# Four graph layers over one 2048-node adjacency: diagonal products of the first and fourth chunk one place later, the mask counts and row checks set apart, and S2 before S3 in the second column block

## The chip, the cores and the metric

The kernel runs on one core of a Trainium2 chip (trn2). The time is the device time of one execution in microseconds (us). Three runs of the kernel before gave 1041.26, 1042.79 and 1042.98 us, median 1042.79 us. TensorE is called PE, VectorE DVE, ScalarE ACT, GpSimd POOL and SyncE SP.

## The reference, cut to what matters

Activations `x` are 8 batches x 2048 nodes x 64 channels; `adj` is a 2048 x 2048 row-normalised 0/1 matrix. Four layers follow each other, each with a residual and a layer norm:

```python
x = ln(x + L0(x))     # Chebyshev: x, A x, 2 A (A x) - x, times per-node weights
x = ln(x + L1(x))     # attention masked by adj > 0.5
x = ln(x + L2(x))     # ((A + I) (x W^T + b)) / rowsum
v = x with node 0 replaced
for _ in range(3):    # L3
    v = relu([v, A v] W1^T + b1) W2^T + b2
x = ln(x + v)
```

No entry of this `adj` is above 0.5, so every attention row is a uniform mean over the nodes. The kernel uses that and proves it while it runs: it counts the mask entries per row, compares them with the count of entries in the rows of `adj` as read from memory, looks for entries above the diagonal's value, and branches to a general program when anything differs. A count, a check and a branch are therefore part of the computation.

## The kernel before, in words

**Data.** The 512 columns (batch x channel) are four chunks `c` of 128; the 2048 nodes are four blocks `j` of 512. `Bm` holds the mask as fp8, `S` the stationary operand as a high and a low fp16 half, `T` the results as high and low halves, `X` the running activations in fp32. Every fp32 tensor that PE reads is split in two steps: ACT copies it to fp16 (high half), then POOL or DVE writes the rest (low half).

**Order.** Nothing is scheduled at run time. Two Python functions, `middle_order` and `last_order`, make one list of steps, and each engine walks through it and does its own part of each step, waiting on semaphores. So a step early in the list stands in front of everything after it on *each* of its engines. In `last_order`, `at(y, ...)` puts steps at half product number y: products `P` 1 to 15 have two halves each, and the steps of y = 2k stand before the first half of product k, those of 2k + 1 before its second. From y = 32 on the places are the half slots h = y - 32 of the last layer (`on(h, ...)`).

**The steps that the change and the prediction touch.**
- `P k` (L788): a 512-column product of layer 2, 32 matmuls of 512 columns, k = 4c + j, and 8 small ones (L938). Product k uses PSUM bank k mod 3.
- `E k`: ACT copies the bank to T (high half), DVE makes the low half. `W c j` (L773 to L775, 12 matmuls) is the weight product; it waits for the low half of E k with k = 4c + j, and stands at y = 2k + 4 (2k + 6 for c = 0), so between two products: `W 1 0` (needs E4) before product 6, `W 1 1` (E5) before 7, `W 1 2` (E6) before 8, `W 1 3` (E7) before 9, `W 2 0` (E8) before 10.
- `split c j`: after DVE has scaled a block (`apply`, L1531), ACT copies it to fp16 and POOL makes the low half.
- `rows`: eight small DVE operations on per-row constants.
- `v0 c j`: the same split for the third pass of the last layer's input; `D c j` (L763, L764, 8 matmuls) multiplies that input by the diagonal matrix `dg` and waits for POOL's low half.
- `G`, `M`, `t22`, `V`: the last layer as one level of a seven-product block scheme with slots `X11, X12, S2, S1, S3, S4, X22`. `G` is a weight product, `M` the product with the mask (L955), `mix` makes the sums S1 to S4 on DVE (L1598), `cut` splits each into halves on ACT and POOL.
- `chk it` (16 of them): ACT copies row tile `it` of the mask, 128 x 2048 fp8, with an accumulated sum into `cnt`. `sgn it` (16): ACT makes two passes over a row tile of `adj` in fp32: Relu (over the diagonal) with its sum into `over`, then Sign with its sum into `sg1`. There is one landing buffer `rowt` for those rows, which SP refills (1 MB) after each Sign, and one scratch output `junk`, which `chk` and the Relu share.
- `flags`, `total`, `verdict`: DVE, PE and DVE again turn the sums into the branch flag. The branch stands before h = 56.

Before, one list entry `chk` and one `sgn` alternate: `chk` at y = 12, 16, 20, 24, 28, 32, then every 4 less a little; `sgn` two places after each. The last `sgn` is at h = 40, `flags` at 44, `total` at 46 and `verdict` at 47.

Of the kernel before, what the change touches and what calls it, by code (L numbers as in the profile page):

```python
# [177 lines left out]
def last_order(after):  # L178


    order = []
    late, half, between = {}, {}, {}

    def at(y, *steps):

        (late if y < 32 else half).setdefault(y if y < 32 else y - 32, []).extend(steps)

    def on(h, *steps):
        half.setdefault(h, []).extend(steps)

    for k in sorted(after):
        at(int(2 * k), *after[k])
    for c in range(NC):
        for j in range(4):
            y = 2 * (4 * c + j)
            at(y + (6 if c == 0 else 4), ("W", c, j))
            at(y + (8, 6, 6, 5)[c], ("sq", 2, c, j), ("red", 2, c, j))
        y = (15, 21, 31, 36)[c]
        at(y, ("var", 2, c))
        at(y + 1, ("root", 2, c), ("rs", 2, c), ("apply", 2, c, 0), ("apply", 2, c, 1), ("v0t", c))  # L200
        at(y + 2, ("apply", 2, c, 2), ("apply", 2, c, 3), ("v0", c, 0))
        at(y + 3, ("v0", c, 1), ("v0", c, 2))
        at(y + 4, ("v0", c, 3))
        y += c > 0
        at(y + 5, ("D", c, 0), ("D", c, 1))
        at(y + 6, ("D", c, 2), ("D", c, 3))
    at(8, ("rows",))
    for i in range(48, 64):
        at(i - 46, ("bt", i))

    for n, y in ((2, 26), (3, 40)):
        at(y, *take(n, 0, "X11", "X12"))
        at(y + 1, cut(n, 0, "X11"), *take(n, 1, "X11", "X12"), cut(n, 0, "X12"))
        at(y + 2, cut(n, 1, "X11"), cut(n, 1, "X12"))
    for n, y in ((2, 29), (3, 45)):
        at(y, *take(n, 0, "X21", "X22"))
        at(y + 1, *mixes(n, 0, 1, 3, 2), cut(n, 0, "X22"), cut(n, 0, "S2"))
        at(y + 2, cut(n, 0, "S3"), *mixes(n, 0, 4), *take(n, 1, "X22"), cut(n, 0, "S1"))
        at(y + 3, cut(n, 0, "S4"), *take(n, 1, "X21"))
        at(y + 4, *mixes(n, 1, 1, 3, 2), cut(n, 1, "X22"), cut(n, 1, "S2"))  # L220
        at(y + 5, *mixes(n, 1, 4), cut(n, 1, "S1"))
        at(y + 6, cut(n, 1, "S3"), cut(n, 1, "S4"))
    for it in range(NT):
        at(12 + 4 * it if it < 5 else 32 + 4 * (it - 5) - (it - 5) // 4, ("chk", it))
        at(14 + 4 * it if it < 5 else 34 + 4 * (it - 5) - (it - 5) // 4, ("sgn", it))
    for k in range(16):
        p = pieces("P", k)
        order += late.pop(2 * k, []) + (p[0:2] if k else []) + late.pop(2 * k + 1, []) + (p[2:4] + [("E", k)] if k else [])
    for n in (4, 5, 6, 7):
        h = 14 * (n - 3)  # L230
        on(h + 2, *take(n, 0, "X11"))
        on(h + 3, *take(n, 0, "X12"), cut(n, 0, "X11"))
        on(h + 4, *take(n, 0, "X21"), cut(n, 0, "X12"))
        on(h + 5, *take(n, 0, "X22"))
        on(h + 6, *mixes(n, 0, 1, 3, 2), cut(n, 0, "X22"))
        on(h + 7, cut(n, 0, "S2"), *mixes(n, 0, 4), *take(n, 1, "X11"))
        on(h + 8, cut(n, 0, "S4"), cut(n, 0, "S1"), *take(n, 1, "X22"))
        on(h + 9, cut(n, 1, "X11"))
        on(h + 10, cut(n, 0, "S3"), *take(n, 1, "X12"))
        on(h + 11, cut(n, 1, "X12"), *take(n, 1, "X21"))  # L240
        on(h + 12, *mixes(n, 1, 1, 3, 2), cut(n, 1, "X22"))
        on(h + 13, cut(n, 1, "S2"), *mixes(n, 1, 4))
        on(h + 14, cut(n, 1, "S1"))
        on(h + 15, cut(n, 1, "S3"))
        on(h + 16, cut(n, 1, "S4"))
    on(44, ("flags",))
    on(46, ("total",))
    on(47, ("verdict",))

    for n, s, jj, h in ((6, 1, 0, 61), (6, 1, 1, 62), (6, 4, 0, 69), (6, 4, 1, 70), (6, 5, 0, 71), (6, 5, 1, 72), (6, 6, 0, 72),  # L250
                        (6, 6, 1, 73), (7, 1, 0, 75), (7, 1, 1, 76), (7, 4, 0, 80), (7, 4, 1, 81)):
        on(h, ("F", *ending(n, s, jj)), ("sq", 3, *ending(n, s, jj)))
    def outs(n, s):
        return [("out", *ending(n, s, jj)) for jj in range(2)]

    for n, s, h in ((6, 1, 64), (6, 4, 71), (6, 5, 74), (6, 6, 75), (7, 1, 77)):
        u = ending(n, s, 0)
        on(h, ("var3", *u), ("root3", *u), ("rs3", *u), *outs(n, s))

    r, (u, v), (x, y) = ending(7, 4, 0), [ending(7, 5, jj) for jj in range(2)], [ending(7, 6, jj) for jj in range(2)]  # L260
    on(82, ("var3", *r), ("root3", *r), ("F", *u), ("sq", 3, *u), ("rs3", *r), *outs(7, 4))
    on(83, ("F", *v))
    between[83] = [("F", *x), ("sq", 3, *v), ("red", 3, *v), ("var3", *u)]
    on(84, ("root3", *u), ("rs3", *u), *outs(7, 5), ("F", *y), ("sq", 3, *x), ("red", 3, *x), ("sq", 3, *y), ("red", 3, *y), ("var3", *x), ("root3", *x),
       ("rs3", *x), *outs(7, 6))
    on(57, ("fin",))
    for h in range(85):
        if h == 56:
            order.append(("branch",))
        order += half.get(h, [])  # L270
        if h < 84:
            n, s, jj = 2 + h // 14, h % 14 // 2, h % 2
            if s == 3:
                order.append(("t22", n, jj))
            order += [("M", n, s, 2 * jj)] + between.get(h, []) + [("M", n, s, 2 * jj + 1), ("V", n, s, jj)]
    return order
# [16 lines left out]
def cut(n, jj, what):  # L293
    return "cut", n, jj, what
# [7 lines left out]
def gnn_kernel(nc, x_in, at_in, a_in, embt_in, sm_in, bx_in, w0_in, a12_in, w0bb_in, out):  # L302
    ctx = ExitStack()
    with ctx:
# [376 lines left out]
                    RSN[norm_key(x)] = len(RSN)  # L681

        number_norms()

        ORDER3 = [ending(n, s, jj) for n in (6, 7) for s in ENDS for jj in range(2)]

# [379 lines left out]
        def scalar_steps(e, steps):  # L1066
# [3 lines left out]
            for step in steps:  # L1070
# [91 lines left out]
                elif kind == "cut":  # L1162
                    n, jj, what = step[1:]
                    if what[0] == "X":
                        e.wait_ge(s_ut, GN[(n // 2, *block_of(n, jj, what))] + 1)
                    else:
                        e.wait_ge(s_mx, MN["mix", n, jj, what] + 1)

                    if what in ("S1", "S2", "S3"):
                        if n > 2:  # L1170
                            e.wait_ge(s_p, slot_done(n - 1, {"S2": 2, "S1": 3, "S3": 4}[what], 1))
                    elif n >= 4:
                        e.wait_ge(s_p, slot_done(n - 2, [x[0] for x in SLOTS].index(what), 1))
                    else:
                        c, j = block_of(n, jj, "X21" if what == "S4" else what)
                        e.wait_ge(s_d, 4 * c + j + 1)
                    fn(half_of(n, what, 0, jj), four(made(n, jj, what)), ACT.Copy).then_inc(s_uh, 1)
                elif kind == "v0":
                    c, j = step[1:]
                    e.wait_ge(s_p, 4 * c + 4)  # L1180
                    e.wait_ge(s_n[2], 4 * c + j + 1)
                    if j == 0:
                        e.wait_ge(s_vt, c + 1)
                        fn(stile(0, 0, c), V0T, ACT.Copy)
                        fn(S[:, 0, 1:4, chunk(c)], X[:, 1:4, chunk(c)], ACT.Copy).then_inc(s_vh, 1)
                    else:
                        fn(spart(0, c, j), xpart(c, j), ACT.Copy).then_inc(s_vh, 1)
                elif kind == "D":
                    c, j = step[1:]
                    e.wait_ge(s_d, 4 * c + j + 1)  # L1190
                    fn(T[:, c, 0, block(j)], bank(aux_bank[step]), ACT.Copy, scale=1.0 / EDGE).then_inc(s_dh, 1)
                elif kind == "chk":
                    it = step[1]
                    e.wait_ge(s_zp, 8 * NT)
                    if it:
                        e.wait_ge(s_over, it)
                    fn(junk, Bm[:, it, :], ACT.Copy, accum_out=cnt[:, it:it + 1]).then_inc(s_cnt, 1)
                elif kind == "sgn":

                    it = step[1]  # L1200
                    e.wait_ge(s_land, 16 * (it + 1))
                    e.wait_ge(s_nr, 1)
                    e.wait_ge(s_cnt, it + 1)
                    fn(junk, rowt, ACT.Relu, bias=nr[:, it:it + 1], accum_out=over[:, it:it + 1]).then_inc(s_over, 1)
                    e.wait_ge(s_over, it + 1)
                    fn(rowt, rowt, ACT.Sign, bias=nr[:, it:it + 1], accum_out=sg1[:, it:it + 1]).then_inc(s_sign, 1)

# [1054 lines left out]
```

## Time and profile before

| | before |
|---|---|
| device time, median of 3 (us) | 1042.79 |
| profiled execution: time (us) | 1043.06 |
| profiled execution: span of the profile (us) | 1041.3 |
| mean granted PE clock, share of full | 0.994 |
| PE busy / DVE / ACT / POOL (us) | 1012.3 / 678.1 / 456.8 / 552.9 |
| share of the span | 97% / 65% / 44% / 53% |

The span runs from the first to the last instruction; 1.8 us lie around it. Busy shares are averages over stages with different limits. PE is busy nearly always, so what can move the time is a stretch in which PE stands still, or in which its clock is lower. ACT is busy for 44% of the whole, and that share differs much from stage to stage.

### The profile page before, as it was taken

How to read it: one execution, taken by the hardware profiler on the slowest of the kernel's cores; microseconds unless marked ns; L12 is line 12 of the kernel's file. 1: busy time of each engine (PE TensorE's matmuls, PEld its weight loads, DVE VectorE, ACT ScalarE, POOL GpSimd, SP SyncE). 2: the span in 40 equal slices, each digit the busy share in tenths (PEclk: the TensorE clock that was granted, in tenths of full speed). 3: DMA queues.
4: the chain of work that ended last, by engine and by line, in shares of the span. 5: the costliest groups of instructions: out<-in, count | busy, mean ns of one | idle time of the engine just before them, and what ended most of it. 6: DMA issues, size and time to landing. Idle time of an engine off the chain costs nothing. (4 is left out here: it accounts for less than half of the span.)

```text
span 1041.3 us, 18648 instructions
## 1 busy us (share of the span) xinstructions
PE 1012.3 (97%) x6854; PEld 486.3 (47%) x6854; DVE 678.1 (65%) x1683; ACT 456.8 (44%) x1109; POOL 552.9 (53%) x645
## 2 busy tenths in 40 slices
PE   7999999999999999999999999999999999999995
PEld 3445444444444444434445556454554545455553
DVE  4877565657566786687667775776584545547556
ACT  4632323333334543444333575584766532232632
POOL 0005497766658798879878374464443242323311
PEclk9999999999999999999999999999999999999998
DMA  9930000000000000000010121121221100000022
GB/s 371 404 127 1 2 1 2 1 2 1 1 1 2 2 1 2 1 2 1 1 42 1 41 82 42 41 82 41 82 82 50 72 1 2 3 2 21 21 62 61
DMA packets 14658, 45.65 MB, mean 44 GB/s; under 512 B 960, under 2 KB 9280, under 8 KB 10080
## 3 DMA queue, kind: packets, MB, share of 16 engines
q1 hardware_dynamic: 14560, 44.39, 11.5%
q8 instruction: 56, 0.92, 0.4%
q14 instruction: 42, 0.34, 0.1%
HBM read 40.19 MB, written 4.19 MB: 43 GB/s over the span
## 5 line engine op out<-in xcount | busy, mean ns | idle before, releaser
L788 PE MATMUL PS<-BW,S 128*128 128x512 fp8e4 x1280 | 291.9, 380 | 0.7 <-DVE R L1219 0.7
L1068 ACT ACTIVATE T<-PS,SM 128x128 f32<-128x128 f32 x384 | 112.8, 365 | 234.3 <-DVE X L1219 155.9
L918 PE MATMUL PS<-WZ,R 64*128 64x512 f16 x1536 | 198.0, 377 | 1.2 <-ACT T L1068 1.2
L788 PEld LDWEIGHTS PS<-BW,S 128*128 128x128 f16 x1280 | 120.6, 98 | 150.3 <-issue 18.2
L955 PE MATMUL PS<-BW,S 128*128 128x512 fp8e4 x768 | 173.1, 379 | 0.6 <-POOL T L1737 0.6
L1737 POOL TENSOR_TENSOR T<-T 128x128 f32<-128x128 f32 (+1 forms) x192 | 124.3, 647 | 74.4 <-ACT T L1068 64.3
L1219 DVE SCALAR_TENSOR_TENSOR X<-PS,SM,X 128x128 f32<-128x128 f32 x320 | 109.5, 342 | 76.4 <-PE PS L918 76.4
L918 PEld LDWEIGHTS PS<-WZ,R 64*128 64x128 f16 x1536 | 69.5, 94 | 104.1 <-issue 26.3
L955 PEld LDWEIGHTS PS<-BW,S 128*128 128x128 f16 x768 | 73.7, 98 | 83.9 <-issue 1.1
L955 PE MATMUL PS<-BW,T 128*128 128x512 fp8e4 x480 | 109.5, 379 | 1.3 <-POOL T L1737 1.3
L1737 POOL TENSOR_TENSOR S<-R,S 128x512 f16<-128x512 f32 (+1 forms) x46 | 52.3, 1144 | 105.6 <-ACT S L1068 105.5
L1219 DVE SCALAR_TENSOR_TENSOR T<-PS,SM,T 128x128 f32<-128x128 f32 x256 | 87.7, 343 | 27.1 <-PE PS L918 27.1
L918 PE MATMUL PS<-WZ,T 64*128 64x512 f16 x768 | 103.8, 376 | 0.0
L1737 POOL TENSOR_TENSOR T<-R,T 128x512 f16<-128x512 f32 x40 | 49.3, 1240 | 87.6 <-DVE T L1211 44.8
L1219 DVE SCALAR_TENSOR_TENSOR R<-PS,cs,R 128x512 f32<-128x512 f32 x48 | 36.0, 749 | 64.1 <-PE PS L955 32.7
L1761 POOL TENSOR_TENSOR BW<-BW 128x512 fp8e4<-128x512 fp8e4 x64 | 70.9, 1113 | 2.7
L955 PEld LDWEIGHTS PS<-BW,T 128*128 128x128 f16 x480 | 46.2, 98 | 54.4 <-POOL T L1737 1.8
L1219 DVE SCALAR_TENSOR_TENSOR R<-PS,ra,R 128x128 f32<-128x128 f32 x176 | 48.8, 342 | 33.6 <-PE PS L775 21.8
L1068 ACT ACTIVATE R<-PS,cs 128x512 f32<-128x512 f32 x48 | 32.6, 679 | 83.7 <-PE PS L782 52.5
L1068 ACT ACTIVATE WZ<-WZ,ra 128x2048 f16<-128x2048 f32 (+1 forms) x32 | 63.9, 1996 | 1.3 <-DMA WZ<-a_in 0.8
L1737 POOL TENSOR_TENSOR X<-X,T 128x128 f32<-128x128 f32 x128 | 58.4, 457 | 10.0
L773 PE MATMUL PS<-hat,T 128*128 128x128 f16 x320 | 57.8, 221 | 4.2 <-DVE T L1219 2.5
(210 smaller groups left out, 1518.9 us busy)
## 6 DMA issues: line engine op xcount, KB each, us to landing
WZ<-a_in SPq DMA_DIRECT2D x16, 1024.0 KB, 4.8
BW<-at_in SPq DMA_DIRECT2D x8, 1024.0 KB, 18.4
R<-at_in SPq DMA_DIRECT2D x7, 1024.0 KB, 12.7
out<-X SPq DMA_DIRECT2D x16, 256.0 KB, 2.3
X<-x_in SPq DMA_DIRECT2D x3, 1024.0 KB, 19.6
T<-w_in SPq DMA_DIRECT2D x1, 1536.0 KB, 15.4
R<-at_in SPq DMA_DIRECT2D x2, 512.0 KB, 4.7
SM<-sm_in SPq DMA_DIRECT2D x1, 520.5 KB, 17.9
```

The costliest lines, as they stand in the source:

```text
L773: e.matmul(ok, th, hat[:, 0, kind, :], start=True, stop=False)
L788: m = e.matmul(o, stile(h, t, c), Bm[:, t, block(j)], start=(t == 0 and h == 0), stop=(last and t == NT - 1 and h == 1))
L918: m = e.matmul(bank(b0 + q), halves[kd][zh][r, :], WZ[r, wh, kd, block(g)], start=(i == 0), stop=(i == 8))
L955: m = e.matmul(o, half_of(n, what, h, q % 2)[:, t, :], b[:, 4 * (q % 2) + t, :], start=(s in (0, 1, 3) and q % 2 == 0 and t == 0 and h == ...
L1068: return e.activation(o, i, f, **kw)
L1219: return e.scalar_tensor_tensor(out=o, in0=a, scalar=s, in1=b, op0=f, op1=g)
L1737: return e.tensor_tensor(o, a, b, f)
L1761: e.tensor_tensor(o, a, b, f, saturate=False).then_inc(s_bt, 1)
```

## The change

Four edits, and no instruction is added or taken away:

1. `D` of chunk 0 moves from y = 20, 21 to 21, 22, and `D` of chunk 3 from y = 42, 43 to 43, 44.
2. The list entry `sgn` is cut into `ovr` (the Relu pass) and `sgn` (the Sign pass). All 16 `chk` go to y = 2 to 17, one at each half product. `ovr` 0 to 3 go to y = 10, 13, 16, 19, `ovr` 4 to 15 to y = 51 to 79 (every 2 or 3 places), and each `sgn` one place after its `ovr`. `number_junk` lets each pass that writes `junk` wait for the one before it in the list.
3. In the second column block (jj = 1) of pairs n = 2 and 3, DVE makes S2 before S3, and S2 is cut before X22.
4. `flags`, `total` and `verdict` move from h = 44, 46, 47 to 49, 51, 52.

```diff
-        y += c > 0
+        y += (1, 1, 1, 2)[c]
         at(y + 5, ("D", c, 0), ("D", c, 1))
         at(y + 6, ("D", c, 2), ("D", c, 3))
...
-        at(y + 4, *mixes(n, 1, 1, 3, 2), cut(n, 1, "X22"), cut(n, 1, "S2"))
+        at(y + 4, *mixes(n, 1, 1, 2), cut(n, 1, "S2"), *mixes(n, 1, 3), cut(n, 1, "X22"))
...
-        at(12 + 4 * it if it < 5 else 32 + 4 * (it - 5) - (it - 5) // 4, ("chk", it))
-        at(14 + 4 * it if it < 5 else 34 + 4 * (it - 5) - (it - 5) // 4, ("sgn", it))
+        at(2 + it, ("chk", it))
+        y = 10 + 3 * it if it < 4 else 51 + (13 * (it - 4)) // 5
+        at(y, ("ovr", it))
+        at(y + 1, ("sgn", it))
...
-    on(44, ("flags",))
-    on(46, ("total",))
-    on(47, ("verdict",))
+    on(49, ("flags",))
+    on(51, ("total",))
+    on(52, ("verdict",))
...
+        def number_junk():
+            held = None
+            for x in TAIL:
+                if x[0] in ("chk", "ovr"):
+                    JUNK[x] = held
+                    held = (s_cnt if x[0] == "chk" else s_over, x[1] + 1)
```

What this does to the instruction rows is shown at three places. All line numbers of the changed kernel are 16 higher there.

ACT from the end of the second layer's variances (128x32) on, before. `T<-PS` is an `E`, `S<-X` a `split`, `R<-X` the squares of a norm.

```order
L1068 ACTIVATE T<-T 128x32 [waits s_var] x2
L1068 ACTIVATE T<-PS 128x512 [waits s_p]
L1068 ACTIVATE S<-X 128x4x128 [waits s_n1,s_p2]
L1068 ACTIVATE T<-PS 128x512 [waits s_p]
L1068 ACTIVATE S<-X 128x4x128 [waits s_n1,s_p2]
L1068 ACTIVATE T<-PS 128x512 [waits s_p]
L1068 ACTIVATE S<-X 128x4x128 [waits s_n1,s_p2]
L1068 ACTIVATE R<-X 128x512 [waits s_y2]
L1068 ACTIVATE T<-PS 128x512 [waits s_p]
```

The same place of ACT in the change; `WZ,ra<-BW` is a `chk`.

```order
L1084 ACTIVATE T<-T 128x32 [waits s_var] x2
L1084 ACTIVATE WZ,ra<-BW 128x2048 [waits s_zp]
L1084 ACTIVATE WZ,ra<-BW 128x2048 [waits s_cnt,s_zp]
L1084 ACTIVATE T<-PS 128x512 [waits s_p]
L1084 ACTIVATE S<-X 128x4x128 [waits s_n1,s_p2]
L1084 ACTIVATE WZ,ra<-BW 128x2048 [waits s_cnt,s_zp] x2
L1084 ACTIVATE T<-PS 128x512 [waits s_p]
L1084 ACTIVATE S<-X 128x4x128 [waits s_n1,s_p2]
L1084 ACTIVATE WZ,ra<-BW 128x2048 [waits s_cnt,s_zp] x2
L1084 ACTIVATE T<-PS 128x512 [waits s_p]
```

Two counts stand now in front of each of E1, E2, E3 and E4, where there was none.

ACT from the exponential of the attention row (chunk 3) to E6, before.

```order
L1068 ACTIVATE ROW<-ROW 128x128 [waits s_neg]
L1068 ACTIVATE R<-X 128x512 [waits s_y2]
L1068 ACTIVATE T<-PS 128x512 [waits s_p]
L1068 ACTIVATE R<-X 128x512 [waits s_red,s_y1] x2
L1068 ACTIVATE R<-X 128x512 [waits s_red,s_y2]
L1068 ACTIVATE WZ,ra<-BW 128x2048 [waits s_zp]
L1068 ACTIVATE R<-X 128x512 [waits s_red,s_y1] x2
L1068 ACTIVATE T<-PS 128x512 [waits s_p]
```

The same place in the change; `WZ,ra<-WZ,ra` is an `ovr` or, with only s_over, a `sgn`.

```order
L1084 ACTIVATE ROW<-ROW 128x128 [waits s_neg]
L1084 ACTIVATE R<-X 128x512 [waits s_y2]
L1084 ACTIVATE WZ,ra<-WZ,ra 128x2048 [waits s_cnt,s_nr,s_land]
L1084 ACTIVATE WZ,ra<-BW 128x2048 [waits s_over,s_zp]
L1084 ACTIVATE WZ,ra<-WZ,ra 128x2048 [waits s_over]
L1084 ACTIVATE WZ,ra<-BW 128x2048 [waits s_cnt,s_zp]
L1084 ACTIVATE T<-PS 128x512 [waits s_p]
L1084 ACTIVATE R<-X 128x512 [waits s_red,s_y1] x2
L1084 ACTIVATE R<-X 128x512 [waits s_red,s_y2]
L1084 ACTIVATE WZ,ra<-BW 128x2048 [waits s_cnt,s_zp]
```

Four wide passes stand now between the exponential and E5, where there was none.

PE from the end of product 9 on, before: `dg` rows with s_vl are `D 0 0` and `D 0 1`, the `hat` row is `W 2 0`, and product 10 follows.

```order
L938 MATMUL PS<-dg,S 128x128 x8
L763 MATMUL PS<-dg,S 128x128 [waits s_vl,s_y2]
...
L763 MATMUL PS<-dg,S 128x128 [waits s_vl,s_y2]
...
L773 MATMUL PS<-hat,T 128x128 [waits s_hl,s_zl,s_y2]
...
L788 MATMUL PS<-BW,S 128x512 [waits s_sl,s_zl]
```

The same place in the change.

```order
L954 MATMUL PS<-dg,S 128x128 x8
L789 MATMUL PS<-hat,T 128x128 [waits s_hl,s_zl,s_y2]
...
L804 MATMUL PS<-BW,S 128x512 [waits s_sl,s_zl]
L804 MATMUL PS<-BW,S 128x512 x7
...
L779 MATMUL PS<-dg,S 128x128 [waits s_vl,s_y2]
```

`W 2 0` comes straight after product 9, and `D 0 0` only after the first half of product 10.

## Rows read from the trace of the kernel before

**Rows 1.** The page: busy us, share of the span and instructions of each engine.

```profile
PE 1012.3 (97%) x6854; PEld 486.3 (47%) x6854; DVE 678.1 (65%) x1683; ACT 456.8 (44%) x1109; POOL 552.9 (53%) x645
```

**Rows 2.** Timeline of PE: start us, us, engine line, [idle before <-releaser].

```profile
565.59 7.07 PE L788 MATMUL PS<-BW,S 128*128 128x512 fp8e4 x32
...
572.95 0.22 PE L773 MATMUL PS<-hat,T 128*128 128x128 f16 x1
...
573.62 7.07 PE L788 MATMUL PS<-BW,S 128*128 128x512 fp8e4 x32
...
596.57 0.61 PE L938 MATMUL PS<-dg,S 128*128 128x128 f16 x8
...
600.76 0.22 PE L763 MATMUL PS<-dg,S 128*128 128x128 f16 x1 [3.14 <-POOL S L1737]
...
602.29 4.87 PE L788 MATMUL PS<-BW,S 128*128 128x512 fp8e4 x16
...
607.89 3.62 PE L788 MATMUL PS<-BW,S 128*128 128x512 fp8e4 x16
```

**Rows 3.** Timeline of PE, 668 to 748 us: its four later stops.

```profile
668.49 0.23 PE L773 MATMUL PS<-hat,T 128*128 128x128 f16 x1 [1.69 <-DVE R L1219]
...
686.74 0.39 PE L780 MATMUL PS<-T,hat 128*128 128x512 f16 x1 [0.52 <-DVE T L1219]
...
706.09 0.23 PE L763 MATMUL PS<-dg,S 128*128 128x128 f16 x1 [1.39 <-DVE SM L1219]
...
747.26 1.90 PE L955 MATMUL PS<-BW,T 128*128 128x512 fp8e4 x8 [1.27 <-POOL T L1737]
```

**Rows 4.** Timeline of ACT: one count, and one Relu with its Sign.

```profile
569.39 1.90 ACT L1068 ACTIVATE WZ<-BW 128x2048 f16<-128x2048 fp8e4 x1
...
571.28 0.61 ACT L1068 ACTIVATE R<-X 128x512 f32<-128x512 f32 x1
...
577.40 1.99 ACT L1068 ACTIVATE WZ<-WZ,ra 128x2048 f16<-128x2048 f32 x1
...
579.51 2.00 ACT L1068 ACTIVATE WZ<-WZ,ra 128x2048 f32<-128x2048 f32 x1
```

**Rows 5.** Busy us of each engine in two stretches, with granted clock, DMA share, GB/s.

```profile
538.64:591.49 52.85, 52.85 (x357) 28.56 (x356) 39.26 (x84) 24.23 (x39) 34.87 (x30) 1.00 0.06 21
600.80:610.00 9.20, 9.20 (x62) 5.26 (x63) 4.66 (x10) 7.78 (x12) 6.28 (x6) 0.81 0.31 116
```

**Rows 6.** Timeline of ACT: E1, a split of chunk 2, one of chunk 3, E8.

```profile
538.64 0.58 ACT L1068 ACTIVATE T<-PS 128x512 f16<-128x512 f32 x1
...
545.72 0.63 ACT L1068 ACTIVATE S<-X 128x512 f16<-128x512 f32 x1 [1.42 <-DVE X L1531]
...
584.78 0.63 ACT L1068 ACTIVATE S<-X 128x512 f16<-128x512 f32 x1 [2.69 <-DVE X L1531]
...
591.49 0.58 ACT L1068 ACTIVATE T<-PS 128x512 f16<-128x512 f32 x1
```

**Rows 7.** Timeline of DVE: first of `rows`, low half of E4, one small operation twice.

```profile
552.32 0.53 DVE L1211 TENSOR_SCALAR ra<-ra 128x16 f32<-128x16 f32 x1
...
558.52 0.69 DVE L1219 SCALAR_TENSOR_TENSOR T<-PS,T 128x512 f16<-128x512 f32 x1
...
583.11 0.19 DVE L1518 TENSOR_TENSOR T<-T 128x32 f32<-128x32 f32 x1
...
585.95 0.74 DVE L1518 TENSOR_TENSOR T<-T 128x32 f32<-128x32 f32 x1
```

**Rows 8.** Timeline of POOL, beside the last row of DVE above.

```profile
585.49 1.16 POOL L1737 TENSOR_TENSOR S<-X,S 128x512 f16<-128x512 f32 x1 [10.52 <-ACT S L1068]
```

**Rows 9.** Timelines of ACT and of DVE around 659 us.

```profile
658.95 0.61 ACT L1068 ACTIVATE R<-X 128x512 f32<-128x512 f32 x1
...
659.60 0.69 DVE L1222 TENSOR_REDUCE T<-R 128x8 f32<-128x512 f32 x1 [5.24 <-ACT R L1068]
```

**Rows 10.** The chain that ended last: start us, us, what.

```profile
731.40 2.09 ACT WZ L1068 x2
```

More of the change, by code:

```diff
@@ L683, in gnn_kernel @@
         number_norms()
+        JUNK = {}
+        def number_junk():
[4 more added lines that the diff above has]
+                    held = (s_cnt if x[0] == "chk" else s_over, x[1] + 1)
+        number_junk()
         ORDER3 = [ending(n, s, jj) for n in (6, 7) for s in ENDS for jj in range(2)]
@@ L1194, in scalar_steps @@
                     e.wait_ge(s_zp, 8 * NT)
-                    if it:
-                        e.wait_ge(s_over, it)
+                    if JUNK[step] is not None:
+                        e.wait_ge(*JUNK[step])
                     fn(junk, Bm[:, it, :], ACT.Copy, accum_out=cnt[:, it:it + 1]).then_inc(s_cnt, 1)
-                elif kind == "sgn":
+                elif kind == "ovr":
                     it = step[1]
@@ L1202, in scalar_steps @@
                     e.wait_ge(s_nr, 1)
-                    e.wait_ge(s_cnt, it + 1)
+                    e.wait_ge(*JUNK[step])
                     fn(junk, rowt, ACT.Relu, bias=nr[:, it:it + 1], accum_out=over[:, it:it + 1]).then_inc(s_over, 1)
+                elif kind == "sgn":
+                    it = step[1]
                     e.wait_ge(s_over, it + 1)
```

## The prediction

> **What bounds the kernel now.** I read the busy shares first: PE is busy for 97% of the span [rows 1], so a change of order can gain only PE's stops and what its clock loses, and can lose by making new stops. Next PE's waits and its timeline. In the part that the change touches PE stops five times. The first and longest is at `D 0 1`, 3.14 us, released by POOL, which makes the low half of `v0 0 1` [rows 2]. The others are 1.69 us (a `W` that waits for a PSUM bank from DVE), 0.52, 1.39 (`D 3 0`, a bank again) and 1.27 us (an S2 cut, from POOL) [rows 3], 4.87 us together. After 750 us PE hardly stops until the tail. After the long stop the clock falls: the granted clock of the 9.2 us behind it is 0.81 of full [rows 5], so it was for a part of them at 1.2 GHz, the lower of its two levels; 16 matmuls of 512 columns take 4.87 us there and 3.62 us in the next half product [rows 2]. That is 1.25 us, and it comes with the 3.14 us stop, not with the 1.69 us one.
>
> The third view is ACT's timeline, because most of what the change moves is on ACT. In the 52.85 us from E1 to E8, which are products 3 to 8, ACT is busy for 24.23 us and idle for 28.6 [rows 5, 6].
>
> **Part 1: sixteen counts and three checks in front of E8.** A count takes 1.89 us from its start to the next start, a Relu 2.11, a Sign 2.00 [rows 4]. Between E1 and E8 the kernel before has two counts and one check, 2 x 1.89 + 4.11 = 7.9 us. The change has all sixteen counts and three checks, 16 x 1.89 + 3 x 4.11 = 42.6 us. That is 34.7 us more on an engine with 28.6 us of idle time, and much of that idle time can't be filled, since ACT then waits for DVE to answer its own last result. I follow ACT's queue; its short pieces are read off the same timeline start to start (a copy or square of 512 columns 0.54, a table load 1.28). It is at E1 at 538.64 [rows 6], as before; PE has then all but done product 2, so ACT starts this stretch most of two products behind.
>
> - Two counts (3.78) come first: E1 at 542.4. The split behind it needs DVE's low half, five small operations and the scaling, 2.7 us as after E7 (the wait of 2.69) [rows 6]: 545.7.
> - From there one round is split 0.54, two counts 3.78, the next E 0.57, and a wait of 1.42 for DVE [rows 6], 6.3 us: E2 at 550.0, E3 at 556.3, E4 (with one more square, 0.54) at 563.2. Its low half comes behind DVE's `rows`, which takes 6.2 us before (552.32 to 558.52, where the low half begins) [rows 7]. I take 3.3 us for it and the low half done at 565.2; PE wants `W 1 0` at 564.9 (one W, 0.67 us from 572.95 to 573.62, before 565.59 [rows 2]): a stop of 0.3.
> - E4's end to the split 2.1 us of wait, then split, table load, exponential and a square 2.6, and Relu, count, Sign, count 7.9: E5 at 576.5, low half done at 577.8. PE, 0.35 late, is there at 573.3 (a product and its W take 8.03, from 565.59 to 573.62 [rows 2]): a stop of 4.5.
> - Five squares 2.65, two counts, a Relu and E5 itself: E6 at 585.6, low half 586.9; PE is there at 585.9: 1.1.
> - Table load and its wait 2.4, two squares and E6 1.6, a Sign and two counts 5.8: E7 at 595.4, low half 596.7; PE is there at 595.0: 1.7.
> - E7 0.6, wait 2.7, split, root and square 1.3, Relu and count 4.0, the two copies of `v0 0 0` with a wait 1.5, Sign and count 3.9: E8 at 609.4 (591.49 before [rows 6]), low half 610.7. PE is there at 604.8: a stop of 6.0.
>
> So PE begins product 10 at 611.4 and not at 602.29 [rows 2], 9.1 us later, and the two `D` that it had done by then (0.45 each, 8 matmuls) are still to do: 10.0. The stop in front is longer than 3.14, so the clock falls as before and the 1.25 us stay in both.
>
> Check of E8's 17.9 us another way: 34.7 added less what idle time takes in. The idle time left in my walk is 2.7 + 1.4 + 1.4 + 2.1 + 0.9 + 2.8 + 0.8 = 12.1, so 16.5 of the 28.6 are used, and 34.7 - 16.5 = 18.2.
>
> DVE's `rows` is where the trace leaves a choice. A small DVE operation takes 0.19 us while POOL is idle and 0.74 beside a POOL operation [rows 7, 8], and POOL is busy for 34.87 of these 52.85 us [rows 5]. In the change POOL has nothing to do from about 563.5 on, so the later part of `rows` should run short, hence 3.3. The bounds are 6.2 (all of it slow: everything behind it 2.9 later) and about 2 (0.6 to 1.3 earlier). The Trainium skill, "SBUF — State Buffer", on the port pair that VectorE and GpSimd share, says that one of the two blocks wholly until the other's instruction ends when their accesses clash. By that rule the 6.2 would stay as long as POOL works without a gap, and the sum would be 2.9 higher; if POOL has run dry, it would be mine. The pair 0.19 and 0.74 agrees with a block.
>
> **Part 2: the D of chunks 0 and 3.** The move of chunk 0 takes away the 3.14 us wait for `v0 0 1` only where `v0 0 1` is on time. In the change ACT copies it at 611.9, POOL's low half is there at 615.6, and PE reaches `D 0 1` after half a product, 3.6 us behind 611.4, at about the same time: 0 to 1 us, taken as nothing. So the gain of this edit is already inside the 611.4: the wait for POOL is gone and the wait for E8 stands in its place.
>
> **Part 3: what ACT no longer does from product 10 to pair 3.** Here the change leaves one Sign where the old order has eight counts and eight checks, 8 x (1.89 + 4.11) = 48 us of ACT. That is where the four later stops are. At 658.95 a square starts that had stood behind a Sign of the checks, and DVE had been idle for 5.24 us for it [rows 9]; DVE's lateness then is the bank wait of 1.69. The chain to the last stop goes through a count or check on ACT at 731.40 [rows 10], and S2 before S3 takes another 0.6 from it. With 2 to 4 us of ACT gone in front of each, all four stops of 0.5 to 1.7 us should close: -4.87. Bounds: 0 (DVE is late by itself) and -4.87. I take the whole, as each is shorter than one check.
>
> **Part 4: checks 4 to 15, flags.** They follow each other in 2 or 3 places of about 4.4 us; ACT is then half idle and PE runs without a stop in that region. Once or twice a row that has not landed may hold ACT 2 us. Taken as nothing, bound +1. `verdict` at h = 52 is four slots before the branch: nothing.
>
> **Sum.** +10.0 - 4.87 = +5.1 us. On the profiled execution's 1043.06 (span 1041.3 and 1.8 around it) that makes 1048.2; the median of the runs before is 1042.79, 0.3 lower, which I leave in the range.
>
> **Rivals.**
> *A, the counts fit (faster).* ACT's lost time is idle time that costs nothing, and the counts fill it. If all 28.6 us are used, E8 is late by 34.7 - 28.6 = 6.1, at 597.6, its low half at 598.9; PE is there at 597.0, so product 10 starts at 599.6, 2.7 earlier than before; 0.9 for the two `D`, no stop of 3 us and so no slow clock, -1.25; and the later stops close. -2.7 + 0.9 - 1.25 - 4.87 = -7.9: 1035.1. For it: ACT is only 46% busy there. Against: the waits of 1.42 and 2.7 behind each E are answers from DVE, with the counts placed behind them, not in them. It decides by E8's low half: below about 605.6 the change gains, above it loses.
> *B, the backlog stays (much slower).* As forecast up to product 10, but `rows` stays slow (+2.9) or the later stops don't close (+4.87), because DVE carries the lateness on: 1051.1 to 1053.1, both 1056.0. For it: two of the four are waits for a bank that DVE itself reads [rows 3]. Against: the two that I followed back had a check of ACT in front [rows 9, 10].
> *C, a draw.* ACT recovers about 5 us more than in my walk, E8's low half at 605 to 606: 1043, within 0.2%.
>
> **How the numbers follow.** Forecast 0.52, B 0.23, C 0.10, A 0.15. The time is the forecast's, 1048.2. Its own range is 1045.5 to 1050.5 (2 to 3 us either way for `rows`, `D 0 1` and part 4). The range for 8 in 10 takes in C and most of B, and leaves out A's end: 1040 to 1055. About 0.2% (2.1 us) is what a measurement can tell from no change here: faster 0.15, same 0.09, slower 0.76.
>
> **What the profile after would show.** Right: PE stops in front of `W 1 1`, `W 1 2`, `W 1 3` and `W 2 0` (the `hat` rows between products), released by DVE, the longest at about 605 us and some 6 us long; ACT nearly always busy from 540 to 610; E8 at about 609; low clock behind one or two of these stops; no stop of over 0.5 us between 660 and 760 (counted from the old times). Wrong: no stop at these `W` and E8 before 600 (A); or the stops there, and those at the first `M` of pair 2 and at `D 3 0` there as well (B).

## The result and the profile after

| | before | after |
|---|---|---|
| device time, median of 4 runs each (us) | 1042.52 | 1050.22 (1049.08 to 1050.64) |
| ratio to before, 95% interval | | 1.0076 [1.0061, 1.0091] |
| profiled execution: time / span (us) | 1043.06 / 1041.3 | 1050.43 / 1048.6 |
| mean granted PE clock | 0.994 | 0.990 |

The change makes the kernel slower by 7.7 us in the medians and 7.4 in the profiled executions. The forecast was 1048.2, its own range 1045.5 to 1050.5, and the range for 8 in 10 was 1040 to 1055.

The page after, busy us of each engine, as in [rows 1]:

```profile
PE 1014.9 (97%) x6854; PEld 487.6 (46%) x6854; DVE 671.2 (64%) x1683; ACT 456.7 (44%) x1109; POOL 554.2 (53%) x645
```

ACT has the same work as before, 456.7 us against 456.8. PE has 2.6 us more for the same 6854 matmuls, some of which ran at the lower clock. What changed is where ACT works, and the busy shares don't show it. Two windows do. The first is nearly the stretch from E1 to the old E8 (columns as in [rows 5]: stretch, us, PE, PEld, DVE, ACT, POOL busy, granted clock, DMA share, GB/s). The kernel before:

```profile
538.70:591.00 52.30, 52.30 (x355) 28.25 (x354) 38.77 (x83) 23.68 (x37) 34.81 (x30) 1.00 0.06 21
```

The change, with the second window behind it:

```profile
538.70:591.00 52.30, 46.74 (x300) 24.93 (x299) 24.99 (x60) 42.02 (x53) 30.66 (x27) 0.93 0.06 21
...
673.00:767.00 94.00, 94.00 (x615) 49.87 (x613) 73.02 (x139) 34.84 (x61) 52.83 (x43) 1.00 0.02 7
```

ACT goes from 23.68 to 42.02 us busy, PE from 52.30 to 46.74, and the clock from 1.00 to 0.93. The last line is the pay-back: from 673 to 767 us PE is busy without a gap, where before it had the four later stops [rows 3].

The timeline of PE after, where [rows 2] show before (start, us, engine, line, tiles, idle before it and its releaser). The `hat` rows are the first matmuls of the W in front of products 6 to 10, and all but that of product 8 (589.50) have a stop:

```profile
566.30 0.22 PE L789 MATMUL PS<-hat,T 128*128 128x128 f16 x1 [1.12 <-issue]
...
566.97 7.07 PE L804 MATMUL PS<-BW,S 128*128 128x512 fp8e4 x32
...
578.92 0.26 PE L789 MATMUL PS<-hat,T 128*128 128x128 f16 x1 [4.44 <-issue]
...
580.16 9.07 PE L804 MATMUL PS<-BW,S 128*128 128x512 fp8e4 x32
...
589.50 0.22 PE L789 MATMUL PS<-hat,T 128*128 128x128 f16 x1
...
599.03 0.22 PE L789 MATMUL PS<-hat,T 128*128 128x128 f16 x1 [1.34 <-issue]
...
612.89 0.27 PE L789 MATMUL PS<-hat,T 128*128 128x128 f16 x1 [5.67 <-issue]
...
614.12 5.70 PE L804 MATMUL PS<-BW,S 128*128 128x512 fp8e4 x16
...
620.55 3.62 PE L804 MATMUL PS<-BW,S 128*128 128x512 fp8e4 x16
...
626.01 7.07 PE L804 MATMUL PS<-BW,S 128*128 128x512 fp8e4 x32
```

The four stops are 12.57 us together, and the stop of 3.14 at `D 0 1` is gone. The profile names no engine for them: "issue" is a wait for which it found no releaser. The code names it, as W waits for E's low half on DVE, which follows E on ACT. So the row to read with each stop is the E on ACT just before it. The timeline of ACT after (compare [rows 4, 6]) has two counts in front of E1, the split behind E1, and then E5 and E8:

```profile
538.74 1.89 ACT L1084 ACTIVATE WZ<-BW 128x2048 f16<-128x2048 fp8e4 x1
540.54 0.19 ACT L1084 ACTIVATION_READ_ACCUMULATOR WZ<-BW 128x1 f32 x1
540.81 1.91 ACT L1084 ACTIVATE WZ<-BW 128x2048 f16<-128x2048 fp8e4 x1
...
542.72 0.58 ACT L1084 ACTIVATE T<-PS 128x512 f16<-128x512 f32 x1
...
546.00 0.63 ACT L1084 ACTIVATE S<-X 128x512 f16<-128x512 f32 x1 [2.69 <-DVE X L1550]
...
577.53 0.57 ACT L1084 ACTIVATE T<-PS 128x512 f16<-128x512 f32 x1
...
611.49 0.57 ACT L1084 ACTIVATE T<-PS 128x512 f16<-128x512 f32 x1
```

E5 starts at 577.53, its low half is ready 1.4 us later, and W starts at 578.92. E8 starts at 611.49 and W at 612.89. In this kernel ACT sets PE's pace from product 6 to 10, but for product 8, in front of which PE does not stop. The wait of 2.69 us in front of the split is the other half of the story: the counts stand in front of E, and behind it ACT stands idle until DVE has answered.

### The profile page after: what moved, and what is told of

It is laid out like the page before. It is cut to its first block, busy times and chain, and to the rows that moved or that the text cites. A ratio compares the mean times of both kernels' runs of the same rounds, so it can differ in the third digit from the quotient of the medians.

```text
span 1048.6 us, 18648 instructions
## 1 busy us (share of the span) xinstructions
PE 1014.9 (97%) x6854; PEld 487.6 (46%) x6854; DVE 671.2 (64%) x1683; ACT 456.7 (44%) x1109; POOL 554.2 (53%) x645
## 4 chain that ended last, share of the span: by engine, by line
PE 83%; DVE 6%; ACT 5%; issue 4%; POOL 2%; DMA 0%; ACTq 0%; SPq 0%; POOLq 0%; DVEq 0%
PE PS L971 27%; PE PS L934 22%; PE PS L804 18%; PE PS L856 5%; ACT WZ L1084 3%; PE PS L789 2%; PE PS L791 2%; PE PS L790 2%; DVE X L1550 1%; PE PS L798 1%; PE PS L797 1%; PE PS L796 1%; DVE X L1238 1%; DVE T L1238 1%; PE PS L779 1%
## 5 line engine op out<-in xcount | busy, mean ns | idle before, releaser
L1084 ACT ACTIVATE WZ<-WZ,ra 128x2048 f16<-128x2048 f32 (+1 forms) x32 | 63.7, 1992 | 27.6 <-DMA WZ<-a_in 27.6
```

The source lines that it names most:

```text
L1084: return e.activation(o, i, f, **kw)
```

## The experiments

No experiment leaves out any computation. "Before" is always the kernel before on the same chip.

**Edits 1 and 3 alone** (both D moves and S2 before S3), on the kernel before.

```
-        y += c > 0
+        y += (1, 1, 1, 2)[c]
-        at(y + 4, *mixes(n, 1, 1, 3, 2), cut(n, 1, "X22"), cut(n, 1, "S2"))
+        at(y + 4, *mixes(n, 1, 1, 2), cut(n, 1, "S2"), *mixes(n, 1, 3), cut(n, 1, "X22"))
```

> Edits 1 and 3 alone (D of chunks 0 and 3 one place later, S2 before S3) on the kernel before; counts and checks as before. Theory (the counts and checks in front of E8 are what costs): PE finds no stop at W 1 1 to W 2 0, D 0 1 finds its POOL half ready, so the 3.14 us stop and the slow clock behind it (about 1.7 us together with the small matmuls) go: 5 us less than before, less what the later stops give back because ACT's checks still stand there (they may grow by 1 to 3 us): ratio 0.994 to 0.998. Rival (the moved D or S2 cost something themselves): same or slower than before.

Measured 1035.28 us, ratio 0.9933 [0.9916, 0.9949]: 7.6 us faster, a little more than the 0.994 expected at the most. PE's timeline in this kernel:

```profile
597.91 3.62 PE L788 MATMUL PS<-BW,S 128*128 128x512 fp8e4 x16
...
608.22 0.23 PE L773 MATMUL PS<-hat,T 128*128 128x128 f16 x1 [1.01 <-DVE X L1219]
...
665.51 0.23 PE L773 MATMUL PS<-hat,T 128*128 128x128 f16 x1 [1.70 <-DVE R L1219]
```

Product 10 starts at 597.91 instead of 602.29 [rows 2] and its first half takes 3.62 us instead of 4.87. The stop is gone and the slow clock with it; a stop of 1.01 us comes up behind it. Of the later stops only the first is left. These edits are good by themselves.

**Edits 2 and 4 alone**: the kernel after, with D and S2 as before (the diff above, backwards).

> Edits 2 and 4 alone (counts and checks moved, flags later); D and S2 as before. Theory: E8 at about 611.5 as in the change, and D 0 1, which stands in front of W 2 0 again, now waits for its POOL half until about 617: product 10 is 2 to 3 us later than in the change, later stops mostly closed: 8 to 11 us above before, ratio 1.008 to 1.011. Rival (the loss comes from the moved D or S2): within 0.3% of before.

Measured 1053.55, ratio 1.0109 [1.0093, 1.0126]: 10.7 us slower, as expected. E8 is at 610.47, the stops at W are 1.13, 4.44 and 1.70, there is none between 655 and 770 us, and the two D of chunk 0, still in their old place, wait in turn:

```profile
608.21 0.22 PE L779 MATMUL PS<-dg,S 128*128 128x128 f16 x1 [2.00 <-POOL S L1756]
...
616.92 0.26 PE L779 MATMUL PS<-dg,S 128*128 128x128 f16 x1 [8.11 <-POOL S L1756]
```

So the whole loss is in the counts and checks, and by themselves they close the four later stops. The two parts don't add up: -7.6 and +10.7 would make +3.1, and the change is at +7.7. Beside the checks the D and S2 edits bring 3.3 us (1053.55 to 1050.22) instead of 7.6: E8's stop stands where D's was, and the later stops can be closed only once.

**The parts of edits 1 and 3.** D of chunk 0 alone:

```
-        y += c > 0
+        y += 1
```

> D of chunk 0 alone one place later (y = 21, 22); everything else as in the kernel before. Theory (this edit carries most of the 7.6 us that edits 1 and 3 gain together): the stop of 3.14 us and the slow clock behind it go, 3.3 + 1.7 = 5.0 us, and PE comes 5 us earlier to later stops, which may give 1 to 2 back: 3.5 to 5.5 us below before, ratio 0.995 to 0.9965. Rival (the gain of the two edits is spread evenly, or sits in the later places): ratio above 0.997.

Measured 1038.98, ratio 0.9969 [0.9957, 0.9980], 3.2 us: a little short of the 3.5 to 5.5 expected, and the interval takes in what the theory said and what the rival said. The stop of 3.14 and the slow clock behind it go. The slow clock had cost 1.25 us in the half product and 0.4 in the small matmuls in front of it (1.53 us from 600.76 to 602.29 [rows 2], 1.12 at full clock). Two stops of 1.03 and 0.41 come, and the four later ones stand as they were: 3.14 + 1.66 - 1.44 = 3.4. D of chunk 3 alone:

```
-        y += c > 0
+        y += (0, 1, 1, 2)[c]
```

> D of chunk 3 alone one place later (y = 43, 44). Theory: the stop of 1.39 us goes, and nothing else moves: 1 to 1.6 us below before, ratio about 0.9987, within what can be told from no change. Rival: the two D meet later G in DVE's queue and the stop only moves: ratio 1.000.

Measured 1040.55, ratio 0.9983 [0.9974, 0.9993], 1.6 us, as expected; the stop of 1.39 is the only one that goes. And S2 before S3 alone (the second pair of lines of the first diff):

> S2 before S3 in the second column block of pairs 2 and 3, alone. Theory: the S2 cut of pair 3 is 0.6 to 0.7 us earlier, so the stop of 1.27 us at 747 us falls to about 0.6: ratio 0.9993, no change that can be told. Rival (S3 or X22 are late in their turn): a new stop in pair 2 or 3, ratio 1.001 or more.

Measured 1039.43, ratio 0.9975 [0.9966, 0.9985]. I expected 0.7 us and got 2.7, a miss. Two stops are gone and not one, that of 0.52 at 686.74 too, and D of chunk 3 waits 0.95 instead of 1.39:

```profile
704.34 0.23 PE L763 MATMUL PS<-dg,S 128*128 128x128 f16 x1 [0.95 <-DVE SM L1219]
```

That makes 1.27 + 0.52 + 0.44 = 2.2. The profiled executions are further apart, 3.9 us, but 0.63 of that stands there at product 10's second half (607.26 against 607.89), in front of everything that this edit moves: it is a difference between two executions and no gain of the edit. I had looked at pair 3 only; the same line of code serves pair 2, which probably accounts for the stop of 0.52; that was not tried by itself.

The three parts make 3.2 + 1.6 + 2.7 = 7.5 us of the 7.6 that edits 1 and 3 gain together. The D of chunk 0 does not carry most of it, as I had expected, but less than half: the rival, an even spread, was nearer.

**Checks of rows 0 to 3 behind product 10**, on the kernel after; the counts stay.

```
-        y = 10 + 3 * it if it < 4 else 51 + (13 * (it - 4)) // 5
+        y = (22, 28, 35, 43)[it] if it < 4 else 51 + (13 * (it - 4)) // 5
```

> The change with ovr and sgn 0 to 3 moved from y = 10 to 20 to y = 22, 28, 35, 43 (sgn one behind); all sixteen counts stay at y = 2 to 17. ACT has 12.6 us less in front of E8. Theory (amount of ACT work in front of E8): E8 at about 600 instead of 611.5, the stop at W 2 0 about 3 us, those at W 1 1 to W 1 3 under 1 us each, later stops nearly closed: 3 to 6 us below before, ratio 0.994 to 0.998. Rival (the sixteen counts in front of E1 to E8 are the loss, by their place and not by the sum): still slower than before, 1.003 or more.

Measured 1040.66, ratio 0.9981 [0.9972, 0.9991]. It turns the loss into a gain of 2.2 us, less than the 3 to 6 expected, since E8 and the stop in front of product 10 are later and longer than the 600 and 3 us of the theory. The three checks that went from E8's front cost 9.6 us of time (1050.22 to 1040.66) for 12.3 us of ACT. E8 is at 602.96:

```profile
605.28 0.26 PE L789 MATMUL PS<-hat,T 128*128 128x128 f16 x1 [4.48 <-issue]
```

**One count a product, directly behind E**, with the checks of rows 0 to 3 as in the last.

```
-        at(2 + it, ("chk", it))
-        ... (p[2:4] + [("E", k)] if k else [])
+        ... (p[2:4] + [("E", k), ("chk", k)] if k else [("chk", 0)])
```

> The change with each count k directly behind E k (k = 0 to 15), where ACT waits for DVE's answer before the split, and with the first four row checks at y = 22, 28, 35, 43. Theory (a count costs nothing in the wait between E and split, and 2 us in front of E): E8 within 3 us of the 591.5 of before, no stop at W 1 1 to W 2 0 nor at D 0 1, later stops closed or small: 9 to 11 us below before, ratio 0.989 to 0.992. Rival (each count delays the split and the chain behind it by its whole length): stops of 1 to 2 us at products 8 to 10, ratio 0.995 or more.

Measured 1031.74, ratio 0.9895 [0.9878, 0.9911], as expected and the fastest of all. E8 is at 591.02 and PE has one stop of 0.41 us in the whole stretch. ACT's timeline shows E, the count and the split, back to back:

```profile
543.59 0.58 ACT L1083 ACTIVATE T<-PS 128x512 f16<-128x512 f32 x1
544.07 1.90 ACT L1083 ACTIVATE WZ<-BW 128x2048 f16<-128x2048 fp8e4 x1
...
545.96 0.62 ACT L1083 ACTIVATE S<-X 128x512 f16<-128x512 f32 x1
```

The same with D and S2 in their old places:

> Counts directly behind E k and the first four row checks late, as in e4, but D and S2 in their old places. Theory: counts and checks placed there cost nothing, and ACT relieved between products 10 and pair 3 closes the later stops by itself (they add up to 4.87 us, about 5.5 with the pipeline's refill); the stop at D 0 1 stays (3 us and its slow clock): 4.5 to 6 us below before, ratio 0.994 to 0.996. Rival (the later stops are closed by the moved D and S2, not by ACT's relief): ratio above 0.998.

Measured 1036.69, ratio 0.9950 [0.9934, 0.9967]: met. D's stop stays, the later ones close but for 0.40:

```profile
600.02 0.26 PE L778 MATMUL PS<-dg,S 128*128 128x128 f16 x1 [2.81 <-POOL S L1755]
```

So with the counts in this place the two parts come nearer to adding: 5.5 us here and 7.6 for edits 1 and 3 would make 13.1, and 11.2 are measured. Three of the later stops are in both, and can be closed only once.

**Amount or place?** The kernel with one count behind each E (1031.74) differs from the one with late checks only (1040.66) in two ways: the counts stand behind E, and up to E8 there are half as many. Two more kernels take these apart. Two counts, as many as in the change, directly behind each E:

```
-        ... (p[2:4] + [("E", k)] if k else [])
+        ... (p[2:4] + [("E", k)] + ([("chk", 2*k - 2), ("chk", 2*k - 1)] if k < 9 else []) if k else [])
```

> Two counts, as many as in the kernel after the change, but directly behind each E of products 1 to 8 and not in front of it; Relu and Sign of rows 0 to 3 stand behind product 10, D and S2 as in the change. With two counts in front of E and the same late rows the time was 1040.66 (E8 at 602.96), with one count behind E 1031.74 (E8 at 591.02). Theory 'place': the waits between E and the split (2.7, 1.4, 1.4, 2.2, 0.9, 2.7 us) are filled, so nearly all of the loss goes: E8 at 591 to 594, ratio to the kernel before 0.989 to 0.992, no stop of over 1 us in front of product 10. Theory 'amount': sixteen counts by E8 are too many wherever they stand: E8 at 598 or later, a stop of over 2 us in front of product 10, ratio 0.995 to 0.998.

Measured 1032.93, ratio 0.9907 [0.9892, 0.9923]. E8 is at 592.38. The window of the 52.30 us, and ACT's timeline:

```profile
538.70:591.00 52.30, 52.30 (x350) 28.04 (x348) 35.23 (x81) 41.93 (x54) 34.27 (x30) 1.00 0.00 1
```

```profile
543.16 0.58 ACT L1083 ACTIVATE T<-PS 128x512 f16<-128x512 f32 x1
543.63 1.90 ACT L1083 ACTIVATE WZ<-BW 128x2048 f16<-128x2048 fp8e4 x1
...
545.72 1.91 ACT L1083 ACTIVATE WZ<-BW 128x2048 f16<-128x2048 fp8e4 x1
...
547.63 0.61 ACT L1083 ACTIVATE S<-X 128x512 f16<-128x512 f32 x1
548.14 0.58 ACT L1083 ACTIVATE T<-PS 128x512 f16<-128x512 f32 x1
```

This is the line to set beside the change's: ACT is busy for 41.93 us of the 52.30, there it is 42.02, yet PE is busy for all 52.30 us at a clock of 1.00. "Too many wherever they stand" has fallen. And one count a product in front of E:

```
-        at(2 + it, ("chk", it))
+        at(2 * it + 1, ("chk", it))
```

> One count a product, in front of E (products 0 to 15), the rest as in the other kernel: the amount of the best kernel so far, the place of the change. Theory 'place': a count in front of E still delays it and leaves DVE's answer time empty, E8 at 594 or later, ratio 0.992 to 0.996. Theory 'amount': eight counts (some 16 us) fit into ACT's idle time in front of E too, since ACT then waits for PE at E anyway: E8 at 591 to 592.5, ratio 0.989 to 0.991.

Measured 1033.57, ratio 0.9915 [0.9901, 0.9928], with E8 at 594.28: between what the two theories said. E8 is as late as "place" has it: the count directly in front of it starts at 592.39 and takes 1.89, and without it E8 would stand where it does with two counts behind E. But only small stops follow, of which the largest is this:

```profile
624.28 0.22 PE L789 MATMUL PS<-hat,T 128*128 128x128 f16 x1 [0.72 <-issue]
```

With the late checks, then: two counts in front of E 1040.66 (ratio 0.9981), one in front 1033.57 (0.9915), two behind 1032.93 (0.9907), one behind 1031.74 (0.9895). It takes both, many of them *and* the place in front of E, to lose the 9 us; either remedy gives back most. The intervals of the last three overlap, so which of them is fastest stays open. No kernel has the sixteen counts behind E and the three checks still in front of E8, so what the checks alone cost there is not shown.

## Why the prediction was right, and which terms were off

- **The mechanism held.** The 34.7 us more of ACT in front of E8 delay E8, PE then stops at W, and the later stops close. Two signs came out otherwise: the stops at W are printed "issue" and not with DVE as releaser, and there are four of them and not the walk's five. Undoing the amount or the place takes E8 back from 611.49 to between 591 and 603 and the loss with it. Rival A ("the counts fit") is false for this order, and true for the same counts behind E once the three checks are behind product 10: its condition was that the idle time behind each E can be used, and with two counts behind E nearly all of it is. The forecast had named that: "with the counts placed behind them, not in them". Rival B fell: the later stops closed and `rows` ran short.
- **E8's time was 2.1 us too early** (609.4 against 611.49). From E1 to E8 the walk said 542.4, 550.0, 556.3, 563.2, 576.5, 585.6, 595.4, 609.4, and the trace has 542.72, 550.52, 557.03, 564.07, 577.53, 587.74, 597.63, 611.49. Two terms were mis-sized, by about 1 us each. One is the count, which makes the 1.0 us up to E5. I took 1.89 us start to start from a count followed by something else; a count behind another waits for that one's sum, since both write `junk`, and starts 2.07 later (538.74 to 540.81), five times up to E8, and a count behind a Relu starts 2.17 later and not 2.11. The other is a wait that the walk put at nothing: from E5 to E6 it has 9.1 us and the trace 10.21, because the last of the five squares waits for DVE. It did so before, too; the row of before stands first:

```profile
572.95 0.63 ACT L1068 ACTIVATE R<-X 128x512 f32<-128x512 f32 x1 [1.06 <-DVE T L1222]
```

```profile
583.13 0.63 ACT L1084 ACTIVATE R<-X 128x512 f32<-128x512 f32 x1 [1.06 <-DVE T L1241]
```

- **The stops at W**, forecast 0.3, 4.5, 1.1, 1.7 and 6.0, were 1.12, 4.44, 0, 1.34 and 5.67. Sum 13.6 against 12.57. The third did not come because product 7 ran at the low clock (9.07 us instead of 7.07), so PE came to `W 1 2` at 589.50, when E6's low half was there (from about 589.1 on). So the sum of the stops is near for a reason that the forecast did not have.
- **The slow clock was under-priced.** I kept 1.25 us for it on both sides. It fell twice: behind the stop of 4.44 it cost 2.0 us in product 7 and some 0.6 in W, and behind that of 5.67 product 10's first half took 5.70 us, not 4.87, and its W 1.23 us, from 612.89 to 614.12, not 0.67. So product 10 starts at 614.12 instead of 611.4 (E8 +2.1, W +0.6), and product 11 is 13.55 late (612.46 before, 626.01 after) where the forecast said 10.0: the missing 0.8 is the slow half.
- **`rows`**: 3.3 us forecast within 2 to 6.2, 3.66 measured (561.85 to 565.51). This timeline of DVE after shows its first operation, its last three, and E4's low half:

```profile
561.85 0.42 DVE L1230 TENSOR_SCALAR ra<-ra 128x16 f32<-128x16 f32 x1
...
564.46 0.31 DVE L1231 TENSOR_SCALAR R<-SM,cs 128x64 f32<-128x64 f32 x1
564.81 0.67 DVE L1231 TENSOR_SCALAR R<-c1row,cs 128x64 f32<-128x64 f32 x2
565.51 0.69 DVE L1238 SCALAR_TENSOR_TENSOR T<-PS,T 128x512 f16<-128x512 f32 x1
```

  and this one of POOL its last work before them:

```profile
562.19 2.15 POOL L1780 TENSOR_TENSOR BW<-BW 128x512 fp8e4<-128x512 fp8e4 x2
```

  POOL ends at 564.34, and from there the three operations take 0.98 us. Before, beside POOL, the same three took 1.27 and 2.07 (DVE first, then POOL in the same time):

```profile
555.11 1.27 DVE L1212 TENSOR_SCALAR R<-SM,cs 128x64 f32<-128x64 f32 x1
556.42 2.07 DVE L1212 TENSOR_SCALAR R<-c1row,cs 128x64 f32<-128x64 f32 x2
```

```profile
555.07 1.26 POOL L1737 TENSOR_TENSOR X<-X,bc 128x512 f32<-128x512 f32 x1
556.29 2.15 POOL L1761 TENSOR_TENSOR BW<-BW 128x512 fp8e4<-128x512 fp8e4 x2
```

  DVE's two rows end at 556.38 and 558.49, 0.05 us behind POOL's ends at 556.33 and 558.44. The Trainium skill, "SBUF — State Buffer", section "Who interferes with whom", says that whichever of the two engines issues first gets the shared port pair for its whole instruction and the other blocks fully. These rows agree with that for the last three; no experiment here ran them with POOL alone taken away.
- **The D of chunk 0** bought nothing at its own stop in the change, as forecast. Beside the checks, edits 1 and 3 still bring 3.3 us, since `D 0 0` and `D 0 1` no longer wait in front of W (2.00 and 8.11 with the old places, one wait of 5.67 with the new).
- **The later stops** closed, -4.87 as forecast. It was a little more: pair 2 begins 13.54 us late (659.73 before, 673.27 after) and the branch 7.87 late, so 5.7 came back: each stop cost up to some 0.2 us beside its printed idle time. Why is not shown.
- **Checks 4 to 15**, taken as nothing, cost nothing. ACT waits 27.6 us for rows to land, where the forecast had 2 us once or twice, but PE has no stop from it:

```profile
L1084 ACT ACTIVATE WZ<-WZ,ra 128x2048 f16<-128x2048 f32 (+1 forms) x32 | 63.7, 1992 | 27.6 <-DMA WZ<-a_in 27.6
```

- **The sum.** +13.6 - 5.7 = +7.9 at the branch and at PE's last product with the mask (1026.73 before, 1034.61 after), and +7.4 at the end. The half us lies in PE's last `W`, the first row of before, the second of after:

```profile
1032.34 0.31 PE L775 MATMUL PS<-hat,T 128*128 128x128 f16 x1
```

```profile
1039.81 0.22 PE L791 MATMUL PS<-hat,T 128*128 128x128 f16 x1
```

  PE comes to this W behind a stop of 2.06 us in both kernels; in the profiled execution before, its clock fell there, and in the one after it did not. The change has no part in that. So the error of the forecast is +3.6 at product 11, less 0.8 in the later stops and 0.5 in the tail. Without these two the time would have been about 1051.7; that the median lies inside the forecast's own range, by 0.3 us, is in part luck.

## What to carry to other kernels

Filler work on an in-order engine belongs behind the instruction whose result another engine is waiting for, in the time until the answer comes, and not in front of it: here that was 1040.66 against 1032.93 us (ratios 0.9981 and 0.9907) for the same sixteen counts. With half as many in front of each E little was lost (1033.57), so the place matters where the queue in front has no slack left. Before moving work "into idle time" of an engine, split that time by what it waits for: what lies between a result and its answer is free only to what is issued behind the result. And test the parts of a change apart: here one part was worth -7.6 us and was buried by another at +10.7.

## What the runs showed of the hardware

- PE's clock fell behind some stops and not behind others. Behind 2.81, 3.14, 4.44, 4.48, 5.67 and 8.11 us the next matmuls ran slowly (a half product above 4 us, or a whole one above 8); behind 1.0 to 2.00 us the first took 0.22 or 0.23 and a half product, where one followed, 3.62. Behind the stop of 2.06 us in front of the last W the clock fell in the profiled execution of the kernel before, and not in that of the change.
- The price doesn't grow with the stop. Behind 8.11 us, 20 small matmuls took 2.09 us instead of 1.12 and the half product 4.04 instead of 3.62, 1.4 us in all; behind 5.67, 12 small ones 1.23 instead of 0.67 and the half product 5.70, 2.6 us. Behind the same stop of 3.14 us the half product took 4.87 us in one kernel and 4.06 in another, where the small matmuls in front were the slower ones (2.09 against 1.53).
- A slow stretch can be nearly free: where ACT sets the pace, at full clock PE would have come to `W 1 2` 2.6 us earlier and waited for E6's low half for 2.2 of them.
- "issue" as a releaser can hide a cross-engine wait. All 12.57 us of new stops were printed so, and only the code and ACT's timeline name the cause.
- Two ACT passes that write the same scratch tile with a sum follow each other in 2.07 us, those with other work between them in 1.89: some 0.2 us for each pair in which the kernel lets the second wait for the first.
